# A gather column moved from GpSimd to SyncE, a leaky relu by a maximum, and a projection in halves

## The chip, the cores and the metric

The program runs on one core of a Trainium2 chip. The metric is the device time of one execution in microseconds (us); a kernel's time is the median of its runs. The engines are PE (TensorE), DVE (VectorE), ACT (ScalarE), POOL (GpSimd) and SP (SyncE, which only issues DMAs and waits).

## The reference

Four graph layers run one after the other on the same graph: 12,500 nodes with 64 features, 200,000 edges sorted by their end node `dst`, each with a start node `src`. Each layer gathers a row for every edge by `src`, makes a message from it and an edge attribute, and reduces the messages by `dst`:

```python
# layer 0: 4 heads; q and v rows of src, k of dst
scores = einsum('ehd,ehd->eh', q[edge_src], k[edge_dst]) / sqrt(D)   # softmax over dst, times v[src], summed
# layer 1: 2 heads
h_edge = (atom[src] + bond) @ W                                      # softmax over dst, summed
# layer 2: 1 head
se = concatenate([h[src], eh]);  msg = leaky_relu(se @ W_msg, 0.01)
att = sum((concatenate([qrh, qeh]) @ W_q / temp) * (se @ W_k))       # softmax over dst, alpha * msg summed
# layer 3
msg = relu(concatenate([x[src], edge_32]) @ w1 + b1)                 # mean over dst, then node layers
x = layernorm(x + layer(x))                                          # after every layer
```

## The kernel before, in words

The program alternates edge phases 0 to 3 with node phases. A node phase writes a table with one row per node into HBM (`qv_table` with 128 floats a row, `x_table` 64, `pair_table` 192, `hidden_table` 128); the edge phase after it gathers rows from that table.

In an edge phase the edges lie as 128 partitions x 1568 columns, worked on in 56 chunks of `J = 28` columns. A round `i` is two chunks, `b` = 0 and 1, in two buffers; there are 28 rounds. The work of `EdgePhase`:

- POOL (`gpsimd`, L783) issues one `indirect_dma_start` for each column: 128 rows by 128 indices in the SBUF tile `index[b]`. It waits for the indices (`index_in`) and for the buffer (`rows_free`). Semaphores `gathered[u][c]` count the columns by fours.
- SP (`sync`, function `turn`) waits for a chunk's gathers (L798), loads the indices that the same buffer needs in the next round (L717), waits until the attributes are used (`attr_free`, L51), loads those of the next round (L721), waits until ACT has laid out the sums (`ready`) and stores them (L724).
- DVE makes messages, a running softmax and prefix sums by scans; ACT takes exponentials and lays the sums out (L920, L921).

In edge phase 2 a chunk goes through `weigh` in six pieces, each as soon as its columns are there (L1389 to L1394, PE's product at L1340 beside it). After the last piece DVE frees the buffer, does the softmax (L829 to L855), then the leaky relu in place on `msg`, and multiplies `msg`, read transposed, with the weights in PSUM into `values` (L1407), then five scans (L911):

```python
e.scalar_tensor_tensor(msg[:, :, :], msg[:, :, :], 0.01, msg[:, :, :], ALU.mult, ALU.max)          # L1404
e.tensor_tensor(ph.values(b)[:, 0, :, :], msg[:, :, :].rearrange("p j d -> p d j"),
                bcast(ph.weight[:, 0, :], 1, FD), ALU.mult)                                        # L1407
```

`msg` and `values` are in SBUF, `weight` in PSUM. ACT's part in that phase is the exponentials and the laying out.

Node phase 1 writes `pair_table`. Its last sweep goes over 15 groups of up to 7 node columns in a fixed order of stages (`in_turn`): per group ACT applies the relu (`light`, L2088), PE turns back (`turn_back`, L2035), later `turn_x`, ACT moves (`move_x`, L2094), PE projects with up to four matmuls (`project`, L2053), ACT copies all of it from PSUM (`take_x`, L2102 and L2105), SP stores (L1998).

Of the kernel before, what the change touches and what calls it, by code (L numbers as in the profile page):

```python
# [28 lines left out]
P = 128  # L29
# [4 lines left out]
FD = 64  # L34
HEADS = 8
# [31 lines left out]
class Program:  # L67


    def __init__(self, nc, ins, out, n_nodes, ctx):  # L70
# [10 lines left out]
        self.find_rows, self.find_cols = ins["dst_table"].shape  # L81

# [563 lines left out]
class EdgePhase:  # L646


    def __init__(self, p, layer, ctx, gather_from, gather_into, parts=1, gathered=None, merged=False):
# [32 lines left out]
        self.passed = self.sem("passed")  # L682
        self.bank = self.ps("bank", [P, 512])
# [27 lines left out]
    def sync(self, e, attrs):  # L711
# [18 lines left out]
        def turn(i):  # L730
            for b in (0, 1):
                for c in range(self.parts):
                    self.wait_part(e, i, b, c)
# [6 lines left out]
        for i in range(self.alone):  # L740
            turn(i)
        with e.Fori(self.alone, self.rounds - 1) as i:
            turn(i)
# [21 lines left out]
    def gpsimd(self, e):  # L765
# [3 lines left out]
        for i in range(self.rounds):  # L769
            for b in (0, 1):  # L770
# [9 lines left out]
                for j in range(J):  # L780
                    if J * n + j < done:
                        continue
                    e.indirect_dma_start(self.gather_into(u, j), None, self.gather_from,  # L783
                                         bass.IndirectOffsetOnAxis(ap=now[:, j:j + 1], axis=0))\
                        .then_inc(self.gathered[u][j * self.parts // J], 16)
# [9 lines left out]
    def wait_part(self, e, i, b, c):  # L795
        u, (times, per, more) = self.buffer(i, b)
        columns = 16 * J // self.parts
        e.wait_ge(self.gathered[u][c], at(times, per * columns, more * columns))  # L798
# [490 lines left out]
def edge_phase_2(p):  # L1289
# [8 lines left out]
    with ExitStack() as ctx:  # L1298
# [9 lines left out]
        made, used = ph.sem("made"), ph.sem("used")  # L1308
        ph.split = 3 * rows
# [36 lines left out]
        def _(e):  # L1346
            with e.Fori(0, ph.rounds - 1) as i:
                for b in (0, 1):
                    ph.exponentials(e, i, b, decay)
                    ph.lay_out(e, i, b)  # L1350
            i = ph.rounds - 1
            ph.exponentials(e, i, 0, decay)
            ph.lay_out(e, i, 0)
            ph.exponentials(e, i, 1, cut_decay(0), 0)
            e.wait_ge(cut_summed, 1)
            ph.lay_out_cut(e, lambda to, of: e.activation(to, of, ACT.Copy))
            ph.exponentials(e, i, 1, cut_decay(1), 1)
# [4 lines left out]
        def _(e):  # L1362
# [51 lines left out]
            def part_of_last(more):  # L1414

                i, now = ph.rounds - 1, ph.columns(more)
                for k in range(per):
                    if now.start <= pieces[k].start < now.stop:
                        weigh(i, 1, k)
                e.memset(cut_decay(more)[:, :, :, 0], 0.0)  # L1420
                ph.carry_part(e, i, more)
                ph.running_softmax(e, i, 1, now.start, now.stop)
                m = msg[:, now, :]
                e.scalar_tensor_tensor(m, m, 0.01, m, ALU.mult, ALU.max)
                e.drain()
                ph.wait_decay(e, i, 1, more)
                e.tensor_tensor(ph.by_head(ph.part(more))[:, 0, 0:FD, :], msg[:, now, :].rearrange("p j d -> p d j"),
                                bcast(ph.weight[:, 0, now], 1, FD), ALU.mult)
# [513 lines left out]
def node_phase_1(p):  # L1942
# [5 lines left out]
    with ExitStack() as ctx:  # L1948
# [26 lines left out]
        x_turned, x_moved, x_done, x_taken = ph.sem("x_turned"), ph.sem("x_moved"), ph.sem("x_done"), ph.sem("x_taken")  # L1975
# [11 lines left out]
        def _(e):  # L1987
# [8 lines left out]
            for g in range(groups):  # L1996
                e.wait_ge(x_taken, g + 1)
# [16 lines left out]
        def _(e):  # L2014
# [34 lines left out]
            def project(g):  # L2049
                e.wait_ge(x_moved, g + 1)  # L2050
                after(e, x_taken, g)
                for k in range(firsts[g]):
# [16 lines left out]
            in_turn(groups, (1, turn_back), (8, turn_x), (10, project), per=4)  # L2069

        @block.scalar
        def _(e):
# [17 lines left out]
            def move_x(g):  # L2090
                n = firsts[g]
                e.wait_ge(x_turned, g + 1)
                after(e, x_done, g - 1)
                e.activation(x_t[g % 2][:, 0:n, :], x_ps[:, 0:n, :], ACT.Copy).then_inc(x_moved, 1)  # L2094

            def take_x(g):
                n, one = ph.sizes[g], firsts[g]
                e.wait_ge(x_done, g + 1)
# [490 lines left out]
```

## Time and profile before

| | us |
|---|---|
| median of 3 runs | 9136.01 (9131.16 to 9145.02) |
| profiled execution, device time | 9133.93 |
| its span, first to last instruction | 9132.2 |
| POOL busy | 6676.1 (73%) |
| DVE busy | 5454.6 (60%) |
| ACT busy | 2476.6 (27%) |
| PE busy | 1872.5 (21%) |

The profiled execution's own time lies 1.7 us above its span. A share of busy time is an average over eight phases; POOL's holds no time between its instructions. In a list of groups a line gives the source line, engine, operation, tile written <- tiles read, count, total busy us, mean ns of one, and the idle time of the engine before them with what ended it.

### The profile page before, as it was taken

The numbers are of one execution on the slowest core, as the hardware profiler recorded it, in microseconds if no ns is written. First come the engines' busy times: TensorE is split into PE (matmuls) and PEld (weight loads), VectorE is DVE, ScalarE is ACT, GpSimd is POOL, SyncE is SP. The second block draws the span as 40 slices with busy tenths as digits, with TensorE's granted clock in tenths as the row PEclk, the third lists the DMA queues.
The fourth block names the chain that finished last, engine by engine and source line by source line (L and its number), as shares of the span: only waits on it lengthen the run. The fifth ranks groups of instructions, "written<-read, shape, count | busy, mean of one in ns | idle before, by whom it ended". The sixth has DMA issues, their size and how long they took to land. (4 is left out here: it accounts for less than half of the span.)

```text
span 9132.2 us, 36460 instructions
## 1 busy us (share of the span) xinstructions
PE 1872.5 (21%) x4249; PEld 957.9 (10%) x4249; DVE 5454.6 (60%) x6299; ACT 2476.6 (27%) x2302; POOL 6676.1 (73%) x6997
## 2 busy tenths in 40 slices
PE   3000000000200000000054444444434222222224
PEld 1000000000200000000032222222213101010104
DVE  5365656565657777777727777777766333333335
ACT  0122222232523232323231111111114333333333
POOL 6777777776777777777647777777765777777776
PEclk6555555555555555555576666676667656565656
DMA  8233333333123333333225555555542333333332
GB/s 354 82 108 109 108 109 108 111 106 106 31 91 106 107 108 105 111 102 113 86 79 183 179 175 186 178 175 186 178 138 71 115 121 115 121 115 123 113 123 82
DMA packets 384127, 1146.63 MB, mean 126 GB/s; under 512 B 163424, under 2 KB 194682, under 8 KB 362128
## 3 DMA queue, kind: packets, MB, share of 16 engines
q1 hardware_dynamic: 127984, 676.77, 19.7%
q0 software_dynamic: 249696, 445.02, 17.7%
q10 hardware_dynamic: 6336, 23.79, 0.7%
q14 instruction: 95, 0.78, 0.0%
q8 instruction: 16, 0.26, 0.0%
HBM read 736.78 MB, written 408.32 MB: 125 GB/s over the span
## 5 line engine op out<-in xcount | busy, mean ns | idle before, releaser
L783 POOL DMA_INDIRECT pair<-pair_table,edge_ix x1512 | 1480.5, 979 | 460.6 <-issue 460.6
L783 POOL DMA_INDIRECT g<-x_table,edge_ix x1512 | 1427.9, 944 | 460.8 <-issue 460.8
L783 POOL DMA_INDIRECT hidden<-hidden_table,edge_ix x1512 | 1426.7, 944 | 460.8 <-issue 460.8
L783 POOL DMA_INDIRECT qv<-qv_table,edge_ix x1484 | 1400.2, 944 | 452.2 <-issue 452.2
L921 ACT ACTIVATE edge_sums<-edge_val 128x1904 f32<-128x1904 f32 (+3 forms) x220 | 1112.4, 5056 | 459.8 <-DVEq L1535 459.8
L1340 PE MATMUL edge_pair_ps<-w_e,edge_eh_t 128*128 128x384 f32 x1568 | 916.4, 749 | 1101.4 <-DVEq L1393 1086.3
L864 ACT ACTIVATE edge_bank<-edge_weight_arg 128x112 f32<-128x112 f32 (+3 forms) x169 | 38.6, 228 | 3215.0 <-DVE edge_decay_arg L855 3215.0
L911 DVE TENSOR_TENSOR_SCAN edge_val<-edge_bank,edge_val 128x464 f32<-128x464 f32 (+1 forms) x715 | 687.6, 1032 | 358.0 <-ACT edge_val L1497 353.9
L1489 PE MATMUL edge_e_ps<-w_nodes,edge_ea_t 128*128 128x512 f32 x784 | 476.4, 773 | 1465.3 <-DVEq L1529 1456.6
L1528 DVE TENSOR_TENSOR hidden<-hidden,edge_e_ps 128x3584 f32<-128x3584 f32 x55 | 213.8, 3888 | 842.5 <-DMA hidden<-hidden_table,edge_ix 791.9
L1124 DVE TENSOR_TENSOR edge_product<-edge_k_ps,qv 128x896 f32<-128x896 f32 x112 | 185.7, 1658 | 690.7 <-DMA qv<-qv_table,edge_ix 683.4
L1340 PEld LDWEIGHTS edge_pair_ps<-w_e,edge_eh_t 128*128 128x128 f32 x1568 | 419.4, 287 | 1597.8 <-DVEq L1393 1329.5
L1497 ACT ACTIVATE edge_val<-hidden 128x3584 f32<-128x3584 f32 x55 | 348.7, 6340 | 786.7 <-DVEq L1529 786.7
L1389 DVE TENSOR_TENSOR edge_pair_ps<-pair,edge_pair_ps 128x512 f32<-128x512 f32 x336 | 263.8, 785 | 401.1 <-DMA pair<-pair_table,edge_ix 315.0
L911 DVE TENSOR_TENSOR_SCAN edge_val<-edge_decay,edge_val 128x493 f32<-128x493 f32 x448 | 467.4, 1117 | 6.7
L1609 POOL DMA_INDIRECT node_rows<-sums,end_index x392 | 374.4, 955 | 129.5 <-issue 118.2
L1048 PE MATMUL edge_k_ps<-ident,edge_fix_wide 128*128 128x128 f32 x8 | 2.1, 441 | 2091.9 <-DVEq L1008 2091.9
L1048 PE MATMUL edge_bond_ps<-ident,edge_fix_wide 128*128 128x128 f32 x4 | 1.2, 461 | 2043.3 <-DVEq L1008 2043.3
L920 ACT ACTIVATE edge_sums<-edge_peak 128x112 f32<-128x112 f32 (+2 forms) x165 | 50.2, 304 | 1269.9 <-DVEq L1257 669.8
L1489 PEld LDWEIGHTS edge_e_ps<-w_nodes,edge_ea_t 128*128 128x128 f32 x784 | 192.3, 254 | 1749.2 <-DVEq L1529 1502.2
L1228 DVE TENSOR_TENSOR g<-g,edge_bond_ps 128x1792 f32<-128x1792 f32 x56 | 113.2, 2021 | 430.4 <-DMA g<-x_table,edge_ix 394.7
L1246 DVE TENSOR_TENSOR edge_val<-g,edge_bank 128x1792 f32<-128x1792 f32 x112 | 351.6, 3179 | 16.1 <-ACT edge_bank L864 16.1
(430 smaller groups left out, 5730.9 us busy)
## 6 DMA issues: line engine op xcount, KB each, us to landing
sums<-edge_sums SPq DMA_DIRECT2D x56, 1848.0 KB, 7.1
edge_q_in<-in_edge_attr_q SPq DMA_DIRECT2D x56, 1792.0 KB, 9.6
sums<-edge_sums SPq DMA_DIRECT2D x55, 1792.0 KB, 6.3
sums<-edge_sums SPq DMA_DIRECT2D x56, 1008.0 KB, 4.0
sums<-edge_sums SPq DMA_DIRECT2D x55, 924.0 KB, 4.1
edge_k<-k_edges SPq DMA_DIRECT2D x56, 896.0 KB, 4.6
edge_bond<-in_edge_attr SPq DMA_DIRECT2D x56, 896.0 KB, 8.3
edge_eh_t<-in_edge_attr_t SPq DMA_DIRECT2D x56, 896.0 KB, 4.7
```

The costliest lines, as they stand in the source:

```text
L783: e.indirect_dma_start(self.gather_into(u, j), None, self.gather_from, bass.IndirectOffsetOnAxis(ap=now[:, j:j + 1], axis=0))\
L911: return e.tensor_tensor_scan(out=now, data0=keep[:, 0:n, :].rearrange("p f j -> p (f j)"), data1=now, initial=0.0, op0=ALU.mult, op1=ALU.add)
L921: e.activation(self.sums[b][:, :, 0:n], self.val[b][:, :, 1:].rearrange("p f j -> p j f"), ACT.Copy)\
L1124: e.tensor_tensor(product[:, 32 * half:32 * half + 32, :], k_ps[:, :, 1:], q[:, 32 * half:32 * half + 32, :], ALU.mult)
L1228: e.tensor_tensor(g[b][:, :, :], g[b][:, :, :], bond_ps[:, :, :], ALU.add)
L1246: e.tensor_tensor(ph.values(b)[:, n, :, :], rows_now, bcast(ph.weight[:, n, :], 1, FD), ALU.mult)
L1340: last = e.matmul(banks[:, bank, 0:2 * wide], eh_t[b][:, cols.start // 2 + n, :], p.w2_e[:, :], start=True, stop=True)
L1389: e.tensor_tensor(points, two(g[b][:, cols, FD:]), points, ALU.add)
L1489: last = e.matmul(e_banks[:, q, :], ea_t[b][:, q, :], p.w3_e, start=True, stop=True)
L1497: e.activation(ph.val[b][:, :, 1:], g[b].rearrange("p j f -> p f j"), ACT.Relu).then_inc(taken, 1)
L1528: e.tensor_tensor(g[b][:, :, :], g[b][:, :, :], e_ps, ALU.add)
L1609: e.indirect_dma_start(self.rows[:, t, :], None, self.p.sums[self.layer], bass.IndirectOffsetOnAxis(ap=self.p.end_index[:, t:t + 1], axis=0))\
```

## The change

Three edits.

1. **A column by SP.** In all four edge phases, in every second round from the fifth (phase 0) or third (phases 1 to 3) on, POOL leaves out the last column of chunk `b` = 1. SP fetches those 128 rows itself, one DMA a row: it loads up to 22 node numbers at a time into registers (`src_aside`, a new input with those columns' `src`), issues a DMA for each into the tile `aside`, 43 rows in each turn of the round before and 42 in the first turn of the round itself, then waits for all and copies `aside` into column 27 of the buffer (`place`). The last column has semaphores of its own (`last_in`, `placed`), and readers of the last four columns wait for them too.
2. **Leaky relu by a maximum (edge phase 2).** ACT computes `0.01 * msg`, transposed, into `values` (function `damp`), DVE takes the maximum of it and `msg`, read transposed, and then multiplies by the weights in place.
3. **Halves (node phase 1).** `project` and `take_x` each work in two halves (two matmuls or fewer each), with a semaphore for each half.

```diff
+BATCH = 22
+ASIDE = (slice(0, 43), slice(43, 86), slice(86, P))
@@ EdgePhase.sync, turn(i, beside)
                 hold(e, self.attr_free[b], at(i, 1, 1), self.passed)
                 load(b, i * 2 + (2 + b))
+                beside(b)
                 hold(e, self.ready[b], at(i, 1, 1), self.passed)
                 store(b, rows_of(i, b, J))
+        def fetch(k, rows):
+            for first in range(rows.start, rows.stop, BATCH):
+                now = slice(first, min(first + BATCH, rows.stop))
+                _, numbers = p.nc.values_load_multi_w_load_instructions(
+                    p.ins["src_aside"][bass.ds(k + (self.steady + 1) // 2, 1), now],
+                    engines=[mybir.EngineType.SP], min_val=0, max_val=p.n_rows - 1,
...
+                for r, number in zip(range(now.start, now.stop), numbers):
+                    e.dma_start(self.aside[r:r + 1, :], self.gather_from[bass.ds(number, 1), :])\
+                        .then_inc(self.aside_in, 16)
+        def place(i, k):
+            hold(e, self.aside_in, at(k, 16 * P, 16 * P), self.passed)
+            hold(e, self.rows_free[1], at(i, 1, 1), self.passed)
+            u = self.buffer(i, 1)[0]
+            e.dma_start(self.gather_into(u, J - 1), self.aside[:, :]).then_inc(self.placed, 16)
...
-        with e.Fori(self.alone, self.rounds - 1) as i:
-            turn(i)
+        with e.Fori(0, (self.rounds - 1 - self.steady) // 2) as k:
+            one = k * 2 + self.steady
...
+            turn(one, beside_one)            # fetch(k, ASIDE[b])
+            turn(one + 1, beside_two)        # b == 0: fetch(k, ASIDE[2]); place(one + 1, k)
@@ EdgePhase.gpsimd
-                    if J * n + j < done:
+                    if J * n + j < done or (b and j == J - 1 and i in self.with_aside):
                         continue
+    def with_aside(self):
+        return range(self.steady + 1, self.rounds - 1, 2)
@@ edge_phase_2, scalar
+            def damp(i, b, to, now=slice(0, J), more=0):
+                e.wait_ge(joined, at(i, 2, 1 + b + more))
+                e.activation(to, msg[:, now, :].rearrange("p j d -> p d j"), ACT.Copy, scale=0.01).then_inc(damped, 1)
             with e.Fori(0, ph.rounds - 1) as i:
                 for b in (0, 1):
+                    damp(i, b, ph.values(b)[:, 0, :, :])
                     ph.exponentials(e, i, b, decay)
@@ edge_phase_2, vector, chunk
+                e.sem_inc(joined, 1)
                 e.sem_inc(ph.rows_free[b], 1)
                 e.sem_inc(ph.attr_free[b], 1)
                 ph.carry_values(e, i, b)
                 ph.running_softmax(e, i, b)
-                e.scalar_tensor_tensor(msg[:, :, :], msg[:, :, :], 0.01, msg[:, :, :], ALU.mult, ALU.max)
+                values = ph.values(b)[:, 0, :, :]
+                e.wait_ge(damped, at(i, 2, 1 + b))
+                e.tensor_tensor(values, msg[:, :, :].rearrange("p j d -> p d j"), values, ALU.max)
                 e.drain()
                 ph.wait_decay(e, i, b)
-                e.tensor_tensor(ph.values(b)[:, 0, :, :], msg[:, :, :].rearrange("p j d -> p d j"),
-                                bcast(ph.weight[:, 0, :], 1, FD), ALU.mult)
+                e.tensor_tensor(values, values, bcast(ph.weight[:, 0, :], 1, FD), ALU.mult)
@@ node phase 1
-            in_turn(groups, (1, turn_back), (8, turn_x), (10, project), per=4)
+            in_turn(groups, (1, turn_back), (8, turn_x), (10, lambda g: project(g, 0)), (11, lambda g: project(g, 1)), per=4)
...
-                    (11, take_x), per=4)
+                    (11, lambda g: take_x(g, 0)),
+                    (12, lambda g: take_x(g, 1)), per=4)
```

The order of instructions shows this at three places. DVE in edge phase 2, from the end of a chunk's softmax to its scans, before (`edge_msg` is `msg`, `edge_val` is `values`, `edge_bank` holds the weights; a scan is named as its builder's kind):

```order
L855 TENSOR_TENSOR edge_decay_arg<-edge_bank,edge_peak 128x28
L1404 SCALAR_TENSOR_TENSOR edge_msg<-edge_msg 128x1792
L874 ISA
L1407 TENSOR_TENSOR edge_val<-edge_msg,edge_bank 128x64x28
L911 SCALAR_TENSOR_TENSOR edge_val<-edge_bank,edge_val 128x377 x5
```

The same place in the changed kernel:

```order
L928 TENSOR_TENSOR edge_decay_arg<-edge_bank,edge_peak 128x28
L1488 ISA
L1489 TENSOR_TENSOR edge_val<-edge_msg,edge_val 128x64x28
L1492 TENSOR_TENSOR edge_val<-edge_val,edge_bank 128x64x28
L984 SCALAR_TENSOR_TENSOR edge_val<-edge_bank,edge_val 128x377 x5
```

The contiguous instruction on `msg` alone is gone; in its place stands one that reads two SBUF tiles, `msg` transposed, behind a new wait, and the multiplication now reads `values`.

SP in edge phase 2, one chunk's turn, before:

```order
L717 ISA
L717 DMA edge_ix<-in_src 128x28
L721 ISA
L721 DMA edge_eh_t<-in_edge_attr_t 128x1792
L721 ISA
L721 DMA edge_q_in<-in_edge_attr_q 128x3584
L724 ISA
L724 DMA sums<-edge_sums 128x1848
```

The same turn in the changed kernel, to the first row of its first batch (22 pairs like the last two rows follow one another, then the second batch, before `sums` is stored):

```order
L725 ISA
L725 DMA edge_ix<-in_src 128x28
L729 ISA
L729 DMA edge_eh_t<-in_edge_attr_t 128x1792
L729 ISA
L729 DMA edge_q_in<-in_edge_attr_q 128x3584
L753 TENSOR_LOAD in_src_aside_ptr
L753 ISA
L753 REGISTER_ALU
L753 TENSOR_LOAD in_src_aside
L758 ISA
L758 DMA edge_aside<-pair_table 1x192
```

Two register loads and 21 or 22 row DMAs, twice over, now stand between a chunk's attribute loads and its store.

ACT in the last sweep of node phase 1, one group, before:

```order
L2102 ACTIVATE node_pair_out<-node_work 128x1152
L2105 ACTIVATE node_pair_out<-node_work 128x192
L1648 ACTIVATE node_rows<-x_now 128x7x64
L2088 ACTIVATE node_held<-node_held,node_bn 128x512
L2094 ACTIVATE node_x_t<-node_work 128x512
L1658 ACTIVATE node_var<-node_var,eps 128x7
```

The same group in the changed kernel:

```order
L2198 ACTIVATE node_pair_out<-node_work 128x768
L1733 ACTIVATE node_rows<-x_now 128x7x64
L2198 ACTIVATE node_pair_out<-node_work 128x384
L2201 ACTIVATE node_pair_out<-node_work 128x192
L2180 ACTIVATE node_held<-node_held,node_bn 128x512
L2186 ACTIVATE node_x_t<-node_work 128x512
```

The copy of 1152 elements is now one of 768 and one of 384, with the square (L1733) between them.

## Rows read from the trace of the kernel before

**Rows 1.** The page, part 1: busy us, share of the span, instructions.

```profile
PE 1872.5 (21%) x4249; PEld 957.9 (10%) x4249; DVE 5454.6 (60%) x6299; ACT 2476.6 (27%) x2302; POOL 6676.1 (73%) x6997
```

**Rows 2.** The page, part 5: two of the four gather groups.

```profile
L783 POOL DMA_INDIRECT pair<-pair_table,edge_ix x1512 | 1480.5, 979 | 460.6 <-issue 460.6
L783 POOL DMA_INDIRECT g<-x_table,edge_ix x1512 | 1427.9, 944 | 460.8 <-issue 460.8
```

**Rows 3.** Timeline, edge phase 2: start us, us, engine, line, operation.

```profile
5227.35 0.96 DVE L1394 TENSOR_REDUCE edge_bank<-edge_product 128x6 f32<-128x768 f32 x1
...
5229.56 0.95 POOL L783 DMA_INDIRECT pair<-pair_table,edge_ix  x1 [0.30 <-issue]
...
5229.82 2.02 DVE L1404 SCALAR_TENSOR_TENSOR edge_msg<-edge_msg 128x1792 f32<-128x1792 f32 x1
...
5230.81 1.84 POOL L783 DMA_INDIRECT pair<-pair_table,edge_ix  x1 [0.30 <-issue]
5231.98 3.18 DVE L1407 TENSOR_TENSOR edge_val<-edge_msg,edge_bank 128x1792 f32<-128x1792 f32 x1
5232.96 0.95 POOL L783 DMA_INDIRECT pair<-pair_table,edge_ix  x1 [0.30 <-issue]
...
5235.23 4.28 DVE L911 TENSOR_TENSOR_SCAN edge_val<-edge_bank,edge_val 128x377 f32<-128x377 f32 x5
...
5239.57 0.25 ACT L920 ACTIVATE edge_sums<-edge_peak 128x28 f32<-128x28 f32 x1 [8.93 <-DVEq L1412]
```

**Rows 4.** Timeline, start of edge phase 2, before its first chunk.

```profile
4798.70 2.03 DVE L1374 TENSOR_TENSOR edge_msg<-bc_L_gnn_beta,live 128x1792 f32<-128x1792 f32 x1
4799.75 1.79 POOL L783 DMA_INDIRECT pair<-pair_table,first_src  x1 [0.30 <-issue]
```

**Rows 5.** Line L1159 (edge phase 0): ns min/median/max, first and last start.

```profile
L1159 ACT ACTIVATE edge_k_rows<-edge_k x56: 3206/3268/3283, 343.7 to 2224.2; 128x1792 f32<-128x1792 f32 x56
```

**Rows 6.** Timeline, edge phase 1: a chunk's first DVE step, its exponential, what waits for it.

```profile
2998.87 2.02 DVE L1228 TENSOR_TENSOR g<-g,edge_bond_ps 128x1792 f32<-128x1792 f32 x1 [7.28 <-DMA g<-x_table,edge_ix]
...
3011.58 0.22 ACT L864 ACTIVATE edge_bank<-edge_weight_arg 128x56 f32<-128x56 f32 x1 [11.44 <-DVE edge_decay_arg L855]
...
3011.84 6.27 DVE L1246 TENSOR_TENSOR edge_val<-g,edge_bank 128x1792 f32<-128x1792 f32 x2 [0.29 <-ACT edge_bank L864]
```

**Rows 7.** Timeline, node phase 1, last sweep: one group.

```profile
4702.00 1.13 ACT L2102 ACTIVATE node_pair_out<-node_work 128x1152 f32<-128x1152 f32 x1 [3.15 <-PE node_work L2053]
...
4703.24 0.58 ACT L1648 ACTIVATE node_rows<-x_now 128x448 f32<-128x448 f32 x1
4703.70 0.81 ACT L2088 ACTIVATE node_held<-node_held,node_bn 128x512 f32<-128x512 f32 x1
...
4704.57 1.16 PE L2035 MATMUL node_back_ps<-node_centred,node_held 128*128 128x128 f32 x8 [2.17 <-ACT node_held L2088]
...
4705.56 2.75 PE L2053 MATMUL node_work<-w_nodes,node_x_t 128*128 128x384 f32 x8
...
4708.35 1.13 ACT L2102 ACTIVATE node_pair_out<-node_work 128x1152 f32<-128x1152 f32 x1 [3.15 <-PE node_work L2053]
```

**Rows 8.** Timeline of SP, edge phase 2: one turn and the next.

```profile
5224.88 0.33 SPq L717 DMA_DIRECT2D edge_ix<-in_src  x1
5228.72 0.33 SPq L721 DMA_DIRECT2D edge_eh_t<-in_edge_attr_t  x1
5229.34 0.33 SPq L721 DMA_DIRECT2D edge_q_in<-in_edge_attr_q  x1
...
5260.82 0.34 SPq L717 DMA_DIRECT2D edge_ix<-in_src  x1
```

**Rows 9.** Timeline of SP in the setup: DMAs back to back.

```profile
198.86 0.60 SPq L357 DMA_DIRECT2D w_ub<-in_L_gnn_upd_b  x1
199.50 0.60 SPq L357 DMA_DIRECT2D bn_affine<-in_L_gnn_bn_gamma  x1
```

**Rows 10.** DMA issues: KB each, median us from issue to landing.

```profile
edge_ix<-in_src SPq DMA_DIRECT2D x216, 14.0 KB, 1.7
```

More of the change, by code:

```diff
@@ L682, in __init__ @@
         self.passed = self.sem("passed")
+        self.steady = self.alone + 1
+        self.aside = self.sb("aside", [P, p.gather_width[layer]])
+        self.aside_in, self.placed = self.sem("aside_in"), self.sem("placed")
+        self.last_in = self.sem("last_in")
         self.bank = self.ps("bank", [P, 512])
@@ L793, in buffer, with wait_part @@
         return 1 - b, (i, 1, b)
-    def wait_part(self, e, i, b, c):
+    def wait_part(self, e, i, b, c, placed=True):
         u, (times, per, more) = self.buffer(i, b)
         columns = 16 * J // self.parts
-        e.wait_ge(self.gathered[u][c], at(times, per * columns, more * columns))
+        if c < self.parts - 1:
+            e.wait_ge(self.gathered[u][c], at(times, per * columns, more * columns))
+            return
+        if not self.begun:
+            e.wait_ge(self.gathered[u][c], at(i, columns - 16 * b, columns - 16 * b))
+        elif isinstance(i, int) and i < 2:
+            e.wait_ge(self.gathered[u][c], (columns, columns - 16, columns, 2 * columns - 16)[2 * i + b])
+        else:
+            more = columns if b else -16
+            if placed:
+                e.wait_ge(self.gathered[u][c], at(i, columns - 16 * b, more))
+            else:
+                hold(e, self.gathered[u][c - 1], at(i, columns, columns * b), self.passed)
+                hold(e, self.gathered[u][c], at(i, columns - 16 * b, more), self.passed)
+        if b:
+            self.wait_last(e, i, placed)
     def wait_gathered(self, e, i, b):
@@ L1351, in _ @@
             i = ph.rounds - 1
+            damp(i, 0, ph.values(0)[:, 0, :, :])
             ph.exponentials(e, i, 0, decay)
             ph.lay_out(e, i, 0)
+            damp(i, 1, ph.by_head(ph.part(0))[:, 0, 0:FD, :], ph.columns(0))
             ph.exponentials(e, i, 1, cut_decay(0), 0)
@@ L1356, in _ @@
             ph.lay_out_cut(e, lambda to, of: e.activation(to, of, ACT.Copy))
+            damp(i, 1, ph.by_head(ph.part(1))[:, 0, 0:FD, :], ph.columns(1), 1)
             ph.exponentials(e, i, 1, cut_decay(1), 1)
@@ L1419, in part_of_last @@
                         weigh(i, 1, k)
+                e.sem_inc(joined, 1)
                 e.memset(cut_decay(more)[:, :, :, 0], 0.0)
@@ L1996, in _ @@
             for g in range(groups):
-                e.wait_ge(x_taken, g + 1)
+                for half in (0, 1):
+                    after(e, x_taken[half], sum(1 for k in range(g + 1) if halves_of(k)[half]))
                 e.dma_start(table[:, ph.now(g), :], pair_out[g % outs][:, 0:ph.sizes[g], :])\
@@ L2047, in turn_x, with project @@
                 last.then_inc(x_turned, 1)
-            def project(g):
+            def project(g, half):
+                now = halves_of(g)[half]
+                if not now:
+                    return
                 e.wait_ge(x_moved, g + 1)
-                after(e, x_taken, g)
-                for k in range(firsts[g]):
+                after(e, x_taken[half], sum(1 for k in range(g) if halves_of(k)[half]))
+                for k in now:
                     last = e.matmul(pair_banks[:, k, :], x_t[g % 2][:, k, :], p.w2_x, start=True, stop=True)
```

72 lines of the change are left out of this document (52 added, 20 removed).

## The prediction

> **What bounds the kernel now.** I read the page's busy shares first: POOL leads with 6676.1 of 9132.2 us, and DVE, at 5454.6 us, is far from full [rows 1]. A share of 73% proves nothing, so the groups come next. In an edge phase POOL issues 1512 gathers like one another; the idle time before them, 460.8 us, is put down to "issue" alone, so POOL waits for no other engine, and one gather costs 944 ns and 460.8/1512 = 305 ns of issue, 1.249 us [rows 2]. A chunk of 28 columns takes 28 x 1.249 = 35.0 us, a round 70, and the edge phases are that rhythm 28 times over. DVE, ACT, PE and SP follow it. So a gather left out of POOL's stream is worth 1.249 us if nobody else becomes late, and a gather made longer is paid in full.
>
> The second reading is that `pair` gathers are longer in the mean: 979 ns against 944 [rows 2], (979 - 944) x 1512 = 52.9 us in the phase. The timeline shows that it isn't all of them: one gather a chunk takes 1.84 us, its neighbours 0.95 [rows 3]. It starts at 5230.81, while DVE's SCALAR_TENSOR_TENSOR of L1404, both of whose tensor inputs are `msg` in SBUF, runs from 5229.82 to 5231.84; the gather ends at 5232.65, 0.81 us after it. The gather that had begun at 5229.56, 0.26 us ahead of L1404, was not held. A gather needs 0.95 us, so it meets the block about 0.13 us after its start and then has 0.81 us to go. The following L1407, also on `msg` but with its second input in PSUM, holds nobody: the gather at 5232.96 lies inside it and takes 0.95 [rows 3]. A plain TENSOR_TENSOR holds a gather too if both inputs are in SBUF: L1374 ends at 4800.73 and the gather begun inside it ends at 4801.54, again 0.81 later [rows 4]. It follows that POOL today pays 0.90 us a chunk in phase 2 for the leaky relu.
>
> **The change part by part.**
>
> *Gathers removed.* The left-out columns are 12 in phase 0 (rounds 4, 6, ..., 26) and 13 in each of phases 1 to 3: 51 in all. 51 x 1.249 = 63.7 us off POOL's stream. Its loop is written out, so nothing takes their place.
>
> *The maximum.* This is the dearest term. The new L1489 reads `msg` transposed and `values`, both SBUF: by [rows 3, 4] it holds a gather until it ends. How long it takes no row shows. The nearest is L1407, the same transposed read of the same tile, 3.18 us; the other end is the contiguous 2.02 of L1404 [rows 3]. I take 3.18, since it is the transposed read that the two differ in. When it starts: DVE's last reduction ends at 5228.31 [rows 3], then `joined` rises. From the end of a DVE scan to ACT's start lie 5239.57 - 5239.51 = 0.06 us [rows 3], so ACT's `damp` starts at about 5228.4. It is the form of L1159 (1792 elements read transposed, written in rows of 28): 3.27 us [rows 5]; it ends at 5231.67. From an ACT end to the waiting DVE is 3011.84 - 3011.80 = 0.04 us [rows 6]. The maximum runs from 5231.71 to 5234.89. With L1404 gone, gathers start undisturbed at 5230.81 and 5232.06. The second meets the block at 5232.19, is held to 5234.89 and ends at 5235.70 in place of 5233.01: 2.70 us lost, where 0.90 is lost now. That is +1.80 us a chunk, and x 56 = +101 us. The bounds: had the maximum the contiguous 2.02 us, the loss were 1.54, +0.64 a chunk, +36 us; should it start just after a gather's block point, a whole period of 1.25 us less is lost, down to 3.18 - 1.25 = 1.93, +1.03 a chunk, +58 us. A loss of nothing, -52.9 us, is the floor, and 3.18, +128 us, the ceiling at that duration.
>
> The multiplication then reads `values` contiguously with PSUM and holds nobody; the two instructions together take as long as the old pair. DVE waits 1.9 us for `damp` (L1404 could start at 5229.82), which its idle time covers: it hangs on the gathers in the later pieces, and only if a chunk's DVE work outgrew 35 us would that be paid. ACT is busy for 27% [rows 1]. Both at nothing.
>
> *Halves.* In the sweep of node phase 1 a group takes 4708.35 - 4702.00 = 6.35 us, and it is a loop of two engines: ACT copies (4702.00 to 4703.24), squares, applies the relu (4703.70 to 4704.51), PE turns back (from 4704.57), projects (4705.56 to 4708.31), and ACT goes on [rows 7]. In halves ACT starts after two of four matmuls, 2.75/2 = 1.37 us earlier, but must cut its copies: copy 0.7, square 0.5, second copies from 1.40 to 2.0, relu to 2.8, PE 1.0 and 1.37, with 0.1 of hand-overs 5.3 us. That is 1.05 to 1.1 us a group, and over some 14 groups -15 us. Bounds: nothing (the cut costs what it gives) to 14 x 1.37 = -19 us.
>
> *SP's rows.* Between two attribute loads 0.62 us pass, 0.33 of them the DMA [rows 8]; DMAs back to back in the setup come every 0.64 us [rows 9]. A row is a DMA with an address from a register: I take 0.62 us, bounds 0.33 and 0.90 (0.60 for the DMA and 0.29 around it). Two register loads a batch have no row; the nearest is the small index load, 1.7 us to landing [rows 10], so 0 to 3.4 us a batch, and I take 3.4. A turn's fetch is 43 x 0.62 + 6.8 = 33.5 us, behind which stand the store of the sums and the next indices. In phase 2 a turn begins at 5224.88 and its attributes are sent by 5229.7 [rows 8], so SP is through at +38, where the next turn is due at +36 (5260.82), 2 us late, and again; the third fetch (42 rows) begins at about +77 and ends at +110, `aside` lands and is copied by +115, while POOL's own last column of that chunk has landed by +107. DVE waits 8 us in one chunk of four. POOL needs that buffer again only at about +140. Phase 1 is tightest: there the attributes are sent sooner, but DVE frees the buffer only with L1246, which ends at 3018.11, 19 us after the chunk's start at 2998.87 [rows 6], so about 10 us are left. Cost nothing, up to 0.70 us a row (10 us over 128 rows is 0.08).
>
> [...]
>
> **Sum**, against the profiled execution's 9133.9: -63.7 + 101 - 15 = +22, 9156 us. The median of the runs is 2 us higher than that execution; against it 9156 is +0.2%.
>
> **The rivals.**
>
> *The maximum holds no gather.* Then the 52.9 us go too: 9133.9 - 63.7 - 52.9 - 15 = 9002. For it: the instruction is new, and no transposed one with two SBUF inputs stands in the trace. Against it: [rows 3, 4], two kinds of instruction, the same 0.81 us. [...]
>
> *Held, but shorter.* The pair of SBUF inputs runs at the contiguous rate: 9133.9 - 63.7 + 36 - 15 = 9091. Against it: every transposed read here takes 3.2 us [rows 3, 5].
>
> *The next gap.* If `damp` ends 0.48 us later than I say (5232.19 - 5231.71), or the gathers land later beside SP's rows, the maximum begins behind a gather's block point and loses about 2.0: +1.1 x 56 = 62, 9117. For it: 0.48 us is little over a chain of 3.4. Against it: each link of that chain has a row.
>
> *SP too slow.* From 0.70 us a row, `placed` comes so late that POOL waits for `rows_free` in phase 1: at 0.80 us 128 x 0.10 = 12.8 us in each of 13 pairs of rounds, +166 us, 9322; at 0.90 all phases. It decides the sign by itself. For it: bursts at 0.60 us a DMA [rows 9] before any register work. Against it: a DMA of one row has less to describe than 64.
>
> **How the numbers follow.** Chances: the forecast 0.50, next gap 0.14, shorter 0.10, no hold 0.06, SP too slow 0.15, anything else 0.05. The range from 9088 to 9200 takes in the first three and the mild end of SP: just under 0.8. Within the forecast, hand-overs and the duration of the maximum move it by 10 us either way (9146 to 9170). What a measurement can tell from no change is 0.2%, 18 us: 9118 to 9154. Slower: 0.6 of the forecast and nearly all of SP, 0.47. Within: 0.35 of the forecast and half of the gap, 0.27. Faster: the rest, 0.26.
>
> **What will show it.** Right: 51 gathers fewer at 1.25 us spacing; one gather a chunk in phase 2 of 3.6 to 3.7 us that ends 0.81 after L1489; L1489 at 3.2 us, starting 3.4 after the last reduction; groups of node phase 1 at 5.3 us; the other three edge phases 15 to 16 us shorter each. Wrong: a mean `pair` gather under 0.99 us; POOL's idle time put down to `rows_free` or indices; row DMAs further apart than 0.7 us.

## The result, and the profile after

The changed kernel takes 9900.88 us (median of 4 runs, 9899.98 to 9910.96), the kernel before on the same chip 9138.49 (4 runs, 9131.16 to 9145.02). The ratio is 1.0837, with a 95% interval from 1.0818 to 1.0856: 762 us slower, where 22 were forecast. The profiled execution's span is 9899.2 us.

The page, part 5: the four gather groups (busy us, mean ns of one, idle before them and what ended most of it), to be read against [rows 2].

```profile
L825 POOL DMA_INDIRECT pair<-pair_table,edge_ix x1499 | 1543.1, 1029 | 688.6 <-issue 444.8
L825 POOL DMA_INDIRECT g<-x_table,edge_ix x1499 | 1415.4, 944 | 725.6 <-issue 449.0
L825 POOL DMA_INDIRECT hidden<-hidden_table,edge_ix x1499 | 1414.7, 944 | 587.6 <-issue 446.6
L825 POOL DMA_INDIRECT qv<-qv_table,edge_ix x1472 | 1389.6, 944 | 556.3 <-issue 445.4
```

Each group has lost its 13 (or 12) gathers, and a gather still costs 944 ns except in the `pair` group, where the maximum holds some. But the idle time, all of it "issue" before, has grown by 104 to 265 us a group: POOL now waits for others. The waits of edge phase 1 (stretch 2626 to 4842 us; us in total, times, longest) say for whom:

```profile
DVE g L1301 <- DMA g<-edge_aside: 523.8, 13, 42.8
POOL g L825 <- DVEq L1321: 216.7, 15, 18.1
POOL g L825 <- DMA edge_ix<-in_src: 60.2, 12, 5.9
```

DVE waits 13 times, up to 42.8 us, for the column that SyncE copies in, POOL waits for the buffer that DVE then frees late (L1321 raises `rows_free`), and for indices that SyncE sends late. All three hang on SyncE. Its timeline over one pair of rounds of phase 1, from a turn's first DMA to the same one of the next pair:

```profile
3061.61 0.35 SPq L725 DMA_DIRECT2D edge_ix<-in_src  x1
3062.36 0.33 SPq L729 DMA_DIRECT2D edge_bond<-in_edge_attr  x1
3069.14 27.71 SPq L758 DMA_DIRECT2D edge_aside<-x_table  x43
3097.11 0.39 SPq L732 DMA_DIRECT2D sums<-edge_sums  x1
3098.18 0.38 SPq L725 DMA_DIRECT2D edge_ix<-in_src  x1
3098.84 1.08 SPq L729 DMA_DIRECT2D edge_bond<-in_edge_attr  x1
3113.11 27.79 SPq L758 DMA_DIRECT2D edge_aside<-x_table  x43
3141.17 0.39 SPq L732 DMA_DIRECT2D sums<-edge_sums  x1
3142.04 0.36 SPq L725 DMA_DIRECT2D edge_ix<-in_src  x1
3142.80 0.92 SPq L729 DMA_DIRECT2D edge_bond<-in_edge_attr  x1
3156.76 20.93 SPq L758 DMA_DIRECT2D edge_aside<-x_table  x42
3179.01 0.53 SPq L766 DMA_DIRECT2D g<-edge_aside  x1
...
3215.69 0.35 SPq L732 DMA_DIRECT2D sums<-edge_sums  x1
3222.36 0.34 SPq L725 DMA_DIRECT2D edge_ix<-in_src  x1
```

From 3061.61 to 3179.01 there is no pause: 117.4 us in one chain, whose end lets DVE begin the chunk that the column belongs to. And the chain closes on itself: SyncE's program stores that chunk's sums before it begins the next pair, 36.7 us after the copy (3215.69), and reaches the next turn 6.7 us later. So a pair of rounds lasts as long as the fetch and 43.3 us more, 160.7 us here, and this loop through SyncE is the bound: POOL's own pair is 111 gathers of 1.249 us, 138.6.

The view groups the rows of a fetch and leaves its register loads out; they stand in the instructions of L753, over the whole span, and then one by one for the six batches of this pair (ns min/median/max, start):

```profile
L753 SPq TENSOR_LOAD <-in_src_aside_ptr x306: 1062/1150/5683, 526.3 to 9664.7; - x153
L753 SPq TENSOR_LOAD <-in_src_aside x306: 2117/8625/13807, 529.1 to 9666.0; - x153
...
L753 SPq TENSOR_LOAD <-in_src_aside x1: 3154/3154/3154, 3065.8 to 3065.8; - x1
L753 SPq TENSOR_LOAD <-in_src_aside x1: 8461/8461/8461, 3079.5 to 3079.5; - x1
L753 SPq TENSOR_LOAD <-in_src_aside x1: 11671/11671/11671, 3101.3 to 3101.3; - x1
L753 SPq TENSOR_LOAD <-in_src_aside x1: 8491/8491/8491, 3123.4 to 3123.4; - x1
L753 SPq TENSOR_LOAD <-in_src_aside x1: 11491/11491/11491, 3145.1 to 3145.1; - x1
L753 SPq TENSOR_LOAD <-in_src_aside x1: 2126/2126/2126, 3167.5 to 3167.5; - x1
```

A batch costs two loads: an address (1.15 us in the median) and 20 to 22 values, 2.1 to 13.8 us. Added up, the 612 loads take 2852.6 us, 55.9 a pair of rounds. The six batches begin at values 0, 22, 43, 65, 86 and 108 of a table row of 512 bytes, at bytes 0, 88, 172, 260, 344 and 432: only the first and the last start on a multiple of 16, and these two are the cheap ones. In every phase the same two are: by the medians of a phase the first takes 3.0 to 4.8 us, the last 2.2 to 2.3, the four between them 8.3 to 12.6.

### The profile page after: what moved, and what is told of

It reads as the page before. It is cut to its first block and busy times, and to the rows that moved or that the text cites. A ratio compares the mean times of both kernels' runs of the same rounds, so it can differ in the third digit from the quotient of the medians.

```text
span 9899.2 us, 58308 instructions
## 1 busy us (share of the span) xinstructions
PE 1750.7 (18%) x4249; PEld 895.2 (9%) x4249; DVE 5454.3 (55%) x6299; ACT 2657.9 (27%) x2372; POOL 6706.4 (68%) x6946
## 5 line engine op out<-in xcount | busy, mean ns | idle before, releaser
L825 POOL DMA_INDIRECT pair<-pair_table,edge_ix x1499 | 1543.1, 1029 | 688.6 <-issue 444.8
L1414 PE MATMUL edge_pair_ps<-w_e,edge_eh_t 128*128 128x384 f32 x1568 | 793.9, 654 | 1535.5 <-DVEq L1475 1365.5
L1423 ACT ACTIVATE edge_val<-edge_msg 128x1792 f32<-128x1792 f32 (+2 forms) x57 | 182.8, 3207 | 1370.8 <-DVEq L1477 1370.8
L1414 PEld LDWEIGHTS edge_pair_ps<-w_e,edge_eh_t 128*128 128x128 f32 x1568 | 357.9, 248 | 1971.4 <-DVEq L1475 1602.4
```

The costliest lines, as they stand in the source:

```text
L1414: last = e.matmul(banks[:, bank, 0:2 * wide], eh_t[b][:, cols.start // 2 + n, :], p.w2_e[:, :], start=True, stop=True)
L1423: e.activation(to, msg[:, now, :].rearrange("p j d -> p d j"), ACT.Copy, scale=0.01).then_inc(damped, 1)
```

## The experiments

The ratios are to the kernel before, measured on the same chip alongside. The theory, from the loads above: a load of 20 to 22 values is dear if it doesn't start on a multiple of 16 bytes (8.6 us in the median, some 0.4 us a value, against 2.1 for the last one above), and without that excess SyncE's loop would not be the bound. Rivals: the row transfers, the place in the turn, or the maximum.

**One part each.** The three parts of the change, each alone in the kernel before:

```
only_maximum: leaky relu by ScalarE's copy and the maximum; column and halves as before
only_halves:  node phase 1 in halves; the rest as before
only_aside:   SyncE's column of 128 rows; the rest as before
```

> The kernel before with the leaky relu by ScalarE's copy and the maximum alone; column and halves as before. If the trace of the whole change tells the price of the lock (a gather held by the maximum is 2.33 us longer than 944 ns, in place of 0.9 us behind the single pass), the time goes up by about 56 x 1.4 = 77 us, to 9215. As the prediction had it, by 101, to 9239. If most of the 762 us came from this edit (DVE waiting for ScalarE, POOL for DVE), it is above 9400.

> The kernel before with the halves of node phase 1 alone. Prediction's term: 15 us less, 9123. Rival: the group's time is set by another engine, and nothing changes (9138 within 5).

> The kernel before with SyncE's column alone. Theory: the register loads on SyncE (56 us per pair of rounds in the trace of the whole change) make its turn the bound, and nearly all of the loss is here: 9900 - 77 + 15 = 9838, within 25. Rival: the loss needs the maximum too (a turn that would fit beside POOL without it): then below 9500.

Measured: the maximum 1.0102 (1.0086 to 1.0117), +93 us; the halves 0.9976 (0.9966 to 0.9986), -22; the column 1.0802 (1.0786 to 1.0819), +733. The loss is the column's. The three add up to 804 us where 762 were measured, and the column alone lies above the 9838 within 25 that was expected for it (9888, or 9871 by its ratio): in phase 2 its pair of rounds takes (7360.4 - 5380.2)/12 = 165.0 us without the maximum and 167.6 with it (below), so while SyncE's loop is the bound most of the maximum's price is hidden. The maximum costs what the lock costs and nothing behind it: POOL in the kernel with the maximum alone waits for nobody, and its gathers are longer (1043 ns in the mean, 979 before).

```profile
L783 POOL DMA_INDIRECT pair<-pair_table,edge_ix x1512 | 1576.9, 1043 | 460.9 <-issue 460.9
```

One chunk of the changed kernel, on the timeline, is the forecast's picture: ACT's copy for 3.27 us, the maximum for 3.20 behind it, and the gather begun inside it ends 0.79 us after it.

```profile
5310.53 3.27 ACT L1423 ACTIVATE edge_val<-edge_msg 128x1792 f32<-128x1792 f32 x1 [19.41 <-DVEq L1477]
...
5313.83 3.20 DVE L1489 TENSOR_TENSOR edge_val<-edge_msg,edge_val 128x1792 f32<-128x1792 f32 x1 [1.60 <-ACT edge_val L1423]
5314.21 3.61 POOL L825 DMA_INDIRECT pair<-pair_table,edge_ix  x1 [0.30 <-issue]
5318.12 0.95 POOL L825 DMA_INDIRECT pair<-pair_table,edge_ix  x1 [0.30 <-issue]
```

And the halves, on DVE's step of two groups of the last sweep in the kernel with the halves alone (before, a group took 6.35 us [rows 7]):

```profile
4698.10 0.63 DVE L2210 TENSOR_TENSOR x_now<-node_back_ps,x_now 128x448 f32<-128x448 f32 x1 [0.34 <-PE node_back_ps L2039]
...
4703.34 0.62 DVE L2210 TENSOR_TENSOR x_now<-node_back_ps,x_now 128x448 f32<-128x448 f32 x1 [0.34 <-PE node_back_ps L2039]
```

5.24 us a group, where 5.3 was forecast.

**The same fetch in aligned batches.** All 128 rows, the same numbers, the maximum and the halves stay; there is even one batch more:

```diff
-BATCH = 22
-ASIDE = (slice(0, 43), slice(43, 86), slice(86, P))
+BATCH = 20
+ASIDE = (slice(0, 40), slice(40, 80), slice(80, P))
```

> The changed kernel with seven loads (20, 20, 20, 20, 20, 20, 8 values) in place of six (22, 21, 22, 21, 22, 20), so that each starts and ends on a multiple of 16 bytes. Theory: a load whose start and length are multiples of 16 bytes costs 2.2 us as the last of the six did, one that starts elsewhere 0.4 to 0.5 us a value (8.6 to 12 us): the values' loads go from 45 to about 15 us a pair of rounds, SyncE's turn fits again, and the time is between 9150 and 9250 (9138 - 64 + 77 - 15 and what is left of waits). Rival: the last and the first load were short because of where they stand in SyncE's turn, not of their addresses; then the loads stay at 8 to 12 us, and the time within 60 us of 9900.

Measured 0.9993 (0.9984 to 1.0002), and run again beside the kernels below

> The anchor: this kernel had 0.9993 of the time of before where that took 9155 us. If the kernel before takes about 9150 us here, 0.9993 again. [...]

0.9994 (0.9985 to 1.0003). Two constants give back 770 us; the 9148 us lie just under the 9150 to 9250 that were expected. The loads, and two gather groups:

```profile
L753 SPq TENSOR_LOAD <-in_src_aside_ptr x357: 1055/1157/5273, 525.9 to 8886.7; - x179
L753 SPq TENSOR_LOAD <-in_src_aside x357: 884/2191/5930, 528.5 to 8888.0; - x179
```

```profile
L825 POOL DMA_INDIRECT pair<-pair_table,edge_ix x1499 | 1545.0, 1031 | 456.7 <-issue 456.7
L825 POOL DMA_INDIRECT g<-x_table,edge_ix x1499 | 1416.0, 945 | 457.0 <-issue 455.5
```

The median load of values fell from 8.6 to 2.2 us, the loads of a pair of rounds from 55.9 to 29.7, and POOL's idle time is issue alone again. The copy of the column gives the period of a pair of rounds: first and last start, over one less than their count.

The changed kernel:

```profile
L766 SPq DMA_DIRECT2D g<-edge_aside x13: 523/534/535, 2857.6 to 4785.5; - x13
L766 SPq DMA_DIRECT2D pair<-edge_aside x13: 525/531/540, 5365.0 to 7376.5; - x13
```

The batches of 20:

```profile
L766 SPq DMA_DIRECT2D g<-edge_aside x13: 519/525/531, 2734.7 to 4399.1; - x13
L766 SPq DMA_DIRECT2D pair<-edge_aside x13: 523/534/545, 4967.9 to 6744.0; - x13
```

In phase 1 a pair takes (4785.5 - 2857.6)/12 = 160.7 us in the changed kernel and 138.7 here, which is POOL's own. In phase 2 it is 167.6 against 148.0. But nothing is to spare in phase 1: in a pair there the copy is issued 95.5 us after the turn's first DMA (3011.87 - 2916.39), and the 43.3 us behind it are unchanged, 138.8 in all. The place in the turn costs something too. The second and the third load of that pair, of 20 aligned values each, take 2.2 and 4.9 us; the third stands right behind the issue of the attributes:

```profile
L753 SPq TENSOR_LOAD <-in_src_aside x1: 2154/2154/2154, 2932.6 to 2932.6; - x1
L753 SPq TENSOR_LOAD <-in_src_aside x1: 4866/4866/4866, 2947.6 to 2947.6; - x1
```

**The address alone.** The batches of 20 again, and only the table of numbers shifted, so that each load starts 4 bytes past a multiple of 16:

```diff
-    arrays["src_aside"] = np.ascontiguousarray(ends.transpose(1, 0))
+    arrays["src_aside"] = np.ascontiguousarray(np.pad(ends.transpose(1, 0), ((0, 0), (1, P - 1))))
...
-                    p.ins["src_aside"][bass.ds(k + (self.steady + 1) // 2, 1), now],
+                    p.ins["src_aside"][bass.ds(k + (self.steady + 1) // 2, 1), slice(now.start + 1, now.stop + 1)],
```

> The seven loads of 20 (and 8) values again, but with the table of numbers moved by one value (4 bytes), so that every load starts 4 bytes behind a multiple of 16; the same numbers, the same rows. Theory (the address decides): each load of 20 takes 8 to 10 us instead of 2.2 to 3.6, the loads of a pair of rounds together some 65 us, and the time is 9850 to 10050. Rival (the length decides: 20 values are cheap, 21 and 22 dear): the loads stay at 2.2 to 3.6 us and the time at 9148.

> The batches of 20 with the table of numbers moved by 4 bytes. If the kernel before takes about 9150 us here: loads of 8 to 10 us by the address, ratio 1.075 to 1.10 (theory); 0.9993 if only the length mattered. If it takes 10430 us: ratio 1.40 as before.

Its first two runs were on another kind of chip (below); beside the second run of the batches of 20 it was 1.1583 (1.1565 to 1.1600). Its loads and its period:

```profile
L753 SPq TENSOR_LOAD <-in_src_aside_ptr x357: 1040/1132/5258, 524.4 to 10358.7; - x179
L753 SPq TENSOR_LOAD <-in_src_aside x357: 3149/8351/12710, 526.9 to 10360.0; - x179
L766 SPq DMA_DIRECT2D g<-edge_aside x13: 519/525/531, 3030.9 to 5124.1; - x13
```

The same instruction for the same 20 values takes 2.2 us in the median when aligned and 8.4 when not: the address costs some 6 us a load. The place in the turn costs far less (in phase 1 the third and fifth load take 4.9 and 5.0 us in the median aligned, where the second, fourth and sixth take 2.1 to 2.3, and 11.0 and 10.7 at the shifted address, where those take 8.0 to 8.3), and so does the count (aligned, 22 values take 3.2 us as the first load there, 20 take 2.2). The time I gave, 1.075 to 1.10, was a slip of mine: now all seven loads are dear, 69.0 us a pair of rounds where the changed kernel has 55.9, and as SyncE's loop is the bound those 13.1 us are paid in full. The period grows from 160.7 to (5124.1 - 3030.9)/12 = 174.4, by 13.8.

**A version without the lock.** ScalarE writes 0.01 of each piece of the message into that piece's PSUM banks, and the maximum reads it there, so that only one of its inputs is in SBUF:

```diff
-                e.drain().then_inc(used, 1)
+                e.drain().then_inc(joined, 1)
                 e.tensor_reduce(ph.score[:, 0, cols], product[:, 0:slot, :], AX.X, ALU.add)
-                e.drain()
+                e.wait_ge(damped, at(i, 2 * per, per * b + k + 1))
+                e.tensor_tensor(two(msg[:, cols, :]), two(msg[:, cols, :]), values, ALU.max)
+                e.drain().then_inc(used, 1)
...
-                e.scalar_tensor_tensor(msg[:, :, :], msg[:, :, :], 0.01, msg[:, :, :], ALU.mult, ALU.max)
-                e.drain()
```

> The kernel before with the leaky relu piece by piece: ScalarE writes 0.01 of the message into PSUM, and VectorE's maximum reads one input from SBUF and one from PSUM. Theory (only an operation with both inputs in SBUF holds a gather): the 56 gathers of about 1860 ns become 944, 52 us less than before, 0.9943 of it, and no gather over 1000 ns stands behind this line. Rival: VectorE becomes late, since it now waits for ScalarE in every piece; then POOL's idle time put down to rows_free grows, and the time is that of before or more.

> Leaky relu piece by piece through PSUM, all else as before. If the kernel before takes about 9150 us here: 52 us less, ratio 0.9943 (theory), 1.000 or more if VectorE becomes late (rival). At 10430 us: 1.006 again.

On a chip where the kernel before takes 9153 us: 0.9947 (0.9933 to 0.9960), where 0.9943 was expected, and no gather is held behind the maximum any more (those begun inside it take 958 ns at most):

```profile
L783 POOL DMA_INDIRECT pair<-pair_table,edge_ix x1512 | 1433.1, 948 | 460.9 <-issue 460.9
```

**All that gain, together.** Leaky relu through PSUM, the halves, and the column in batches of 20:

> All three that gain together: the leaky relu through PSUM, the halves, and SyncE's column with batches of 20. If the parts add: batches of 20 (-7) without the maximum (-92) and without the single pass's lock (-52): 9155 - 151 = 9004, 0.983 of before. Rival: with POOL shorter by 150 us SyncE's turn is the bound in the phases with the longest rows; then 9030 to 9080.

> Leaky relu through PSUM, halves, and the column with batches of 20. If the kernel before takes about 9150 us here: 151 us less if the parts add, ratio 0.983 to 0.985; 0.987 to 0.993 if SyncE's turn is the bound in a phase. At 10430 us: 1.28 again.

On that chip 0.9951 (0.9938 to 0.9965). It beats both kernels (9108 us) but not leaky relu through PSUM alone (9102, no difference within the intervals), and misses the sum of its parts: 0.9947 - 0.0024 - 0.0084 (the column, worked out below) is 0.9839, 102 us less. The rival, SyncE's turn as the bound in a phase, is borne out in kind, but its 0.987 to 0.993 was too low. Three edge phases kept the column's gain; the one on pair rows didn't. Its waits of POOL (stretch 4742 to 6760 us), and its copies:

```profile
POOL pair L825 <- issue: 475.7, 1530, 9.4
POOL pair L825 <- DVEq L1488: 67.6, 21, 7.1
```

```profile
L766 SPq DMA_DIRECT2D g<-edge_aside x13: 519/525/531, 2738.2 to 4404.7; - x13
L766 SPq DMA_DIRECT2D pair<-edge_aside x13: 523/534/545, 4967.4 to 6718.3; - x13
```

In phase 1 138.9 us a pair, POOL's own; in phase 2 (6718.3 - 4967.4)/12 = 145.9, where the gathers without the lock need 139. In the batches of 20 the lock had hidden this: POOL itself needed 148.0. So here the loop through SyncE is the bound again, by 7 us a pair, 90 in all; DVE waits 161.4 us for the column there.

**The other chips.** Ten runs fell on three chips on which the kernel before takes 10,427 to 10,474 us. Their ratios are kept apart from those above. Beside those already quoted:

> The changed kernel without any register load: the 128 rows of a pair of rounds come from fixed addresses (row 700 + 61 r of the table), so this kernel leaves out reading the numbers and computes with wrong rows in the column. It has the row transfers, the lock and the halves. Theory: 128 row transfers of 0.42 us are 54 us a pair of rounds and fit beside POOL; the time is that of the batches of 20 or up to 20 us less (9128 to 9150). Rival (row transfers themselves take too much of SyncE's turn or slow the gathers): above 9200.

> The same kernel as no_register_loads (fixed row addresses; it leaves out reading the numbers), on a chip as in the first comparisons. Theory: row transfers of 0.42 us fit beside POOL, and without the loads nothing of the loss is left: ratio 0.997 to 1.001, as with the batches of 20 (0.9993). Rival: the row transfers carry part of the loss: above 1.01.

> The same kernel as leaky_in_psum, whose first comparison fell on a chip on which the kernel before took 10435 us and SyncE and GpSimd ran stretches of their programs at one instruction in 0.7 us. On a chip as in the first comparisons: gathers behind the leaky relu 944 ns, 52 us less than before (ratio 0.9943). Rival: VectorE late by its six waits for ScalarE a chunk; then 1.000 or more.

> The same kernel as psum_halves_aside20, on a chip as in the first comparisons: if the parts add, 151 us less than before, ratio 0.983 to 0.985. Rival: SyncE's turn is the bound in some phase; then 0.987 to 0.993. [...]

> The same kernel as off_one (the table of numbers moved by 4 bytes), on a chip as in the first comparisons. The trace on the slow chip had the loads of 20 values at 5.5 to 9.7 us, against 0.8 to 3.8 us for the aligned ones on the same chip. Theory: 8 to 10 us a load here, 65 us a pair of rounds with the pointers, and a time of 1.075 to 1.10 of before, as the changed kernel (1.0837). Rival: loads of 2.2 us and 0.9993.

> Leaky relu through PSUM and the halves, no column on SyncE. The two parts measured alone were 0.9947 and 0.9976; if they add, 0.9923 of before (9083 where before takes 9153). Rival: they overlap nowhere in time, so nothing but addition is expected; a difference over 0.002 would need a new wait.

> psum_halves_aside20 with four batches of 32 values in place of seven (32, 32, and twice 32 in the second round's turn). Theory: in the phase on pair rows SyncE's chain of fetches is the bound (146.0 us a pair of rounds against 139 us that GpSimd needs); three pointer and value loads less take 3.5 to 6 us from it, times 13 pairs 45 to 80 us: 0.9865 to 0.991 of before, so the column then gains 16 us in each of the other phases. Rival: the first load of a batch grows with the batch or the longer fetch delays the attributes; then 0.993 or more.

| kernel | ratio there |
|---|---|
| leaky_in_psum, and again | 1.0059, 1.0070 |
| psum_halves | 1.0045 |
| no_register_loads (fixed rows, it leaves out reading the numbers), and again | 1.0883, 1.0911 |
| psum_halves_aside20, and again | 1.2799, 1.2812 |
| psum_halves_aside32 | 1.2828 |
| off_one, and again | 1.3956, 1.4048 |

The cost of a load by its address is nearly the same there. Values of psum_halves_aside20 (second run):

```profile
L753 SPq TENSOR_LOAD <-in_src_aside x357: 14/2117/5127, 576.2 to 13037.6; - x179
```

and of off_one (second run):

```profile
L753 SPq TENSOR_LOAD <-in_src_aside x357: 3133/8121/11052, 572.5 to 14319.0; - x179
```

What differs is the pace of other instructions on SyncE. The row transfers, in the kernel without register loads (again) there:

```profile
L754 SPq DMA_DIRECT2D edge_aside<-x_table x1664: 1/692/1398, 3210.7 to 5541.2; - x185
```

and in the changed kernel:

```profile
L758 SPq DMA_DIRECT2D edge_aside<-x_table x1664: 217/228/304, 2747.6 to 4784.2; - x185
```

The spacings of instructions heap up at 0.70 and 1.40 us there, in stretches, on SyncE and on POOL. In leaky_in_psum_again 1295 of SyncE's 3897 spacings and 1247 of POOL's 7497 lie within 0.02 us of one of the two, where leaky_in_psum_third, the same kernel, has 5 and 8; ACT has 25 against 29, DVE 218 against 166 of 12,104. The instruction packets of SyncE's long loop don't go with it: the kernel without register loads has nearly those of before (102 packets in part 3 of the page, before has 95, the changed kernel 379) and is slowed all the same (11,381 us, the kernel before 10,427 on that chip). The cause stays open. So do three questions that only these chips answered: what the fetch costs without any register load, whether leaky relu through PSUM and the halves add, and whether four larger batches free SyncE in phase 2.

## Why the prediction failed

*Sign and place.* "Slower" came true by luck: it was forecast for the maximum's lock, which alone costs 93 us, while the column, forecast at -63.7, costs 733. "SP too slow" was among the rivals, at 0.15, and named the right engine, but by row transfers of 0.70 us or more, which aren't there. The forecast, 9156, and its range to 9200 failed.

*The steps that failed* both stand under "SP's rows", and both are about SyncE's column.

The first is a term of the sum: "0 to 3.4 us a batch, and I take 3.4". No row of before held a register load, and I bounded it by a transfer's landing time. Measured, a batch takes 55.9/6 = 9.3 us; 3.4 is about right for an aligned one (1.15 and 2.2). Per value the runs show 0.11 us aligned (2.2/20) and 0.42 not (8.4/20). The ends of the range weren't ends: a bound from a row of another kind of instruction that moves one thing says nothing of one that moves 22. On six batches that is 35.5 us a pair of rounds more. A row transfer was mis-sized the other way, at 0.62 us: its DMA is 0.23 us, and rows follow each other at 0.41 us in the median (27.71 us for 43 rows hold one batch of loads as well), 128 x 0.21 = 27 us a pair less. So the whole fetch of a pair was nearly right: it was forecast to end at +110 in phase 2, or up to 5 us sooner in phase 1, where the attributes are sent earlier, and in phase 1 it ends at +117.4.

The second is the path: "POOL needs that buffer again only at about +140", "so about 10 us are left". That asks when POOL needs the buffer and not when SyncE gets to its next pair. I let its turns begin when they are due; but the sums of the chunk with the column are stored first, and that chunk starts only when the column is there. In the trace of before a chunk of phase 1 starts at 2998.87 [rows 6], and its sums are stored 34.9 us later:

```profile
3033.77 0.35 SPq L724 DMA_DIRECT2D sums<-edge_sums  x1
```

Measured, 43.3 us stand behind the copy in phase 1. Of POOL's 138.6 they leave about 95 for a fetch, so that my own 105 to 110 was already 10 to 15 us too long: by 13 pairs an estimate of 130 to 190 us in phase 1 alone, with 3.4 us a batch and 0.62 a row. The other 7 to 12 of the 22.1 us by which the pair there exceeds POOL's are the fetch, longer than forecast. Aligned loads shorten the fetch to 95.5 us, which is why they give back the whole loss; they do not make the 10 us of room true.

In the 43.3 us is a term that I didn't have, the branch back. Ahead of the pair shown above it stands at 3055.44, and the next instruction comes at 3061.11, 5.7 us later; in the kernel before 0.16 us pass there (3069.00 to 3069.16). Over all of SyncE's branches the median is 5.2 us in the changed kernel (60 branches) and 0.16 before (115). The page's instruction packets went from 95 to 379 beside it; that these make the 5.7 us is not shown.

Over 51 pairs the excess of the periods over those of the batches of 20 makes the loss: with the two other phases, (148.7 - 138.5) x 12 + (160.7 - 138.7) x 13 + (167.6 - 148.0) x 13 + (150.0 - 138.6) x 13 = 811 us, one interval a phase less 748; between the profiled spans of the two kernels lie 753 us, and 770 by their ratios.

*The maximum*, +1.80 us a chunk, +101 us. Mechanism, start, length (3.20 us) and end (0.78 us after it in the median) are as forecast, and measured alone it is +93: the 55 held gathers are 2.64 us longer than 944 ns in the mean, forecast 2.7. In the changed kernel they are 2.34 us longer. Waiting for SyncE isn't needed for that: in the two runs of the batches of 20, where POOL waits for nobody, it is 2.28 and 2.34. The left-out column shifts POOL's beat against DVE's, so that held gathers take between 2.7 and 3.9 us. One detail was wrong: by "meets the block about 0.13 us after its start" a gather begun just ahead of the maximum is held. In the changed kernel 13 gathers began between 0.14 us before and 0.04 us after L1489's start, and each took 0.94 or 0.95 us; those from 0.05 us on were held.

The rival "holds no gather" is refuted: the gather of 3.61 us above is held, and with one input in PSUM none is held behind it (958 ns at most). A gather reads its indices from SBUF (`edge_ix`); which part of its work is held the trace doesn't show.

*The halves*, -15 us: mechanism right, a group 5.24 us for 5.3; measured alone -22 (its interval is from -31 to -13).

*The gathers removed*, -63.7 us: right where SyncE keeps up. Between the batches of 20 and the sum of the other two parts lie 0.9994 - 1.0102 + 0.0024 = -0.0084 of 9138, -77 us, with an error of some 19 us from the three intervals.

## What to carry to other kernels

Price an instruction that has no row in the trace as unbounded above, or measure it alone first, before letting it into a loop whose engine looks idle; an engine with no busy time in the page can still have no time to give. Where work is given to such an engine, follow its program round to where the work begins again, and add what it waits for on the way: here a chunk's whole work, 36.7 us, stood between one fetch and the next, and left 95 us of 139. Where registers are filled from memory, try loads that start on a multiple of 16 bytes: here 20 values then took 2.2 us in place of 8.4, and batches cut so gave back 770 us. And after each bound that is taken away look for the next: the lock had hidden 7 us a pair of the loop through SyncE.

## What was not expected of the hardware

- A load of 20 registers takes 2.2 us in the median at a byte of the table that is a multiple of 16 (0, 80, 160 and so on), 8.4 at one 4 bytes behind it. In the changed kernel starts at 4, 8 and 12 bytes behind a multiple are all dear: by the medians of a phase byte 260 takes 8.3 to 8.8 us, bytes 88 and 344 take 8.5 to 8.8 and 10.6 to 11.5, byte 172 takes 9.5 to 12.6, where byte 432 takes 2.2 to 2.3. With 22 values an aligned load is 3.1 us (phase 0), 0.9 more than with 20 in the same place; unaligned it is 9.1 at least, and 11.5 in phase 1, in places where aligned loads of 20 take 4.9 as well. Whether a count that is no multiple of 4 is what makes 22 dearer is not shown. Loading one address takes 1.1 us, up to 5.7 in phase 2.
- The maximum with one input in PSUM leaves GpSimd's gathers at 948 ns in the mean. With both inputs in SBUF it holds each of the 55 gathers begun inside it from 0.05 us after its start on until 0.78 us after its end, and L1404 of before holds its 55 until 0.82.
- From the branch back of SyncE's long loop to its next instruction 5.7 us pass (at 3055.44; 5.2 in the median), where it is 0.16 us in the kernel before.
- On three of the chips SyncE and GpSimd issue in stretches at 0.70 or 1.40 us an instruction, and of the programs measured on both kinds those with the column suffer most: the kernel before takes 14% more, psum_halves_aside20 47% (13,356 us against 9108), off_one 38% (14,636 against 10,597). Why is open.
